# A gated cross-attention and mixture-of-experts block on one core: head pairs scored as two 64-row halves, both norms' rows turned by DMA, and the router in three bf16 parts

## The reference, cut to what matters

```python
x = x + tanh(g_xattn) * xattn(layernorm(x), ctx)        # x: 32 blocks of 128 rows x 512, fp32
x = x + tanh(g_ffn)  * ffn(layernorm(x))
# xattn, 16 heads, per block of 128 rows:
#   q_r = ((xn @ Wq.T) per head @ w_kc_q) @ W_qr        64 numbers a head
#   k_r = rope(ctx) @ W_kr                              64 numbers a head
#   attn = softmax(q_r k_r^T);  ctx_c = attn @ rope(ctx)
#   out  = (ctx_c @ w_kc_kv^T) @ Wo.T
# ffn: logits = xn @ router (512 x 8); the best 2 of 8 experts a row, 1280 slots an expert,
#   silu(gate) * up, down (352 hidden); plus a shared MLP (1408 hidden) for all rows
```

## Time and profile before

| | |
|---|---|
| time, 3 runs | 2081.36 us median (2079.42 to 2082.54) |
| the profiled execution | 2080.16 us, of which its span is 2078.2 us |
| granted TensorE clock, mean over the span | 0.988 of full speed |
| PE, busy share of the span | 96% |
| DVE, ACT, POOL | 49%, 34%, 28% |
| DMA queue of SP, share of the 16 engines | 30.7% |

### The profile page before, as it was taken

The page is one execution under the profiler, slowest core; times in us unless marked ns, Lnnn a source line. Parts: engine busy times, 40 slices in busy tenths (PEclk is TensorE's granted clock), DMA queues, the critical chain, the costliest instruction groups (busy, mean ns, idle before and its releaser), DMA issues.

```text
span 2078.2 us, 32183 instructions
## 1 busy us (share of the span) xinstructions
PE 1998.2 (96%) x11660; PEld 1170.0 (56%) x11844; DVE 1010.4 (49%) x2011; ACT 710.2 (34%) x1969; POOL 576.1 (28%) x653
## 2 busy tenths in 40 slices
PE   7799999999999999989997999999999999999999
PEld 7466666666666666544444555555554444444444
DVE  5766666666666666636532222222223433242343
ACT  4655555555555566522011222222210000000000
POOL 5633333333333354310011433343302210110101
PEclk9999999999999999999998999999999999999999
DMA  8211111111111131141309998989952731221202
GB/s 279 67 43 49 49 49 48 48 48 48 48 48 48 56 104 57 41 123 46 103 22 209 213 223 216 220 216 223 210 123 77 140 93 36 87 81 26 76 16 87
DMA packets 257551, 207.71 MB, mean 100 GB/s; under 512 B 190640, under 2 KB 196528, under 8 KB 257456
## 3 DMA queue, kind: packets, MB, share of 16 engines
q1 hardware_dynamic: 245936, 168.64, 30.7%
q0 software_dynamic: 11520, 37.76, 6.5%
HBM read 113.02 MB, written 48.23 MB: 78 GB/s over the span
## 4 chain that ended last, share of the span: by engine, by line
PE 83%; DVE 7%; issue 4%; ACT 4%; DMA 1%; POOL 1%; SPq 0%; DVEq 0%; ACTq 0%; POOLq 0%
PE o L552 12%; PE score L705 11%; PE o L789 7%; PE score L778 7%; PE p_bank L606 6%; PE p_bank L705 5%; PE o L716 5%; PE m_bank L705 5%; PE p_bank L778 3%; PE m_bank L778 3%; DVE arena L985 3%; PE c_bank L565 3%; PE score L583 3%; PE t_bank L716 3%; PE c_bank L716 3%
## 5 line engine op out<-in xcount | busy, mean ns | idle before, releaser
L552 PE MATMUL o<-arena 128*128 128x512 bf16 x1472 | 339.0, 379 | 14.8 <-DVE arena L985 12.0
L1363 POOL TENSOR_TENSOR arena<-arena 128x512 f32<-128x512 f32 x128 | 133.5, 1043 | 426.4 <-DVE arena L1001 424.6
L552 PEld LDWEIGHTS o<-arena 128*128 128x128 bf16 x1536 | 148.5, 99 | 169.7 <-DVE arena L985 17.3
L705 PE MATMUL score<-arena 128*128 128x512 bf16 x1035 | 235.5, 381 | 2.5 <-issue 0.7
L825 ACT ACTIVATE arena<-score,arena 128x128 f32<-128x128 f32 x512 | 181.3, 366 | 161.4 <-DVE arena L1025 160.2
L985 DVE TENSOR_TENSOR arena<-p_bank,arena 64x512 bf16<-64x512 f32 (+1 forms) x184 | 126.9, 690 | 141.2 <-ACT arena L875 120.0
L606 PE MATMUL p_bank<-arena 128*128 128x256 bf16 x1536 | 178.8, 273 | 1.8 <-DVE arena L985 1.8
L705 PEld LDWEIGHTS score<-arena 128*128 128x128 bf16 x1056 | 103.6, 98 | 128.0 <-issue 4.1
L778 PE MATMUL score<-arena 128*128 128x352 bf16 x960 | 152.4, 316 | 14.5 <-DMA arena<-arena 14.5
L789 PE MATMUL o<-arena 128*128 128x512 bf16 (+1 forms) x680 | 160.9, 381 | 4.2 <-DMA arena<-arena 2.1
L606 PEld LDWEIGHTS p_bank<-arena 128*128 128x128 bf16 x1536 | 150.4, 98 | 21.0 <-issue 1.7
(11 more groups left out here) (166 smaller groups left out, 3164.0 us busy)
## 6 DMA issues: line engine op xcount, KB each, us to landing
xrow_d<-arena SPq DMA_DIRECT2D x80, 256.0 KB, 3.3
arena<-w_expert SPq DMA_DIRECT2D x32, 544.0 KB, 4.9
arena<-w_shared SPq DMA_DIRECT2D x22, 384.0 KB, 3.6
arena<-x SPq DMA_DIRECT2D x16, 512.0 KB, 3.8
arena<-x SPq DMA_DIRECT2D x32, 256.0 KB, 3.8
x_d<-arena SPq DMA_DIRECT2D x32, 256.0 KB, 2.0
xn_d<-arena SPq DMA_DIRECT2D x32, 256.0 KB, 2.1
arena<-x_d SPq DMA_DIRECT2D x8, 1024.0 KB, 5.8
```

What stands on the lines that cost most here:

```text
L552: mm = pe.matmul(o_bank[b % 2][:, :], lhsT=cT[:, a, h, :], rhs=M_w[:, w, 4 * hg + h, :], start=(hg == 0 and n == 0), stop=(hg == 3 and n = ...
L705: mm = pe.matmul(dst[:, :], lhsT=wsh[m][:, a, col:col + P], rhs=xs[g % 2][:, w, t, :], start=(n == 0), stop=(n == 3 * KT - 1))
L1363: pool.tensor_tensor(prob[:, u % 4], prob[:, u % 4], rden[:, u % 4, :].unsqueeze(2).broadcast_to([P, 4, S]), ALU.mult).then_inc(normed, 1)
```

## The change

- The scores of two units are made together in the even steps. `kT` holds K without the zeros; per head one matmul of 64 rows and 128 columns, the even heads from rows 0 to 63 into `score_bank[0]`, the odd ones from rows 64 to 127 into `score_bank[1]`, in turn. Heads are numbered by `head_of` accordingly. The K pieces' high and low parts become one instruction each over 128 rows, and the memsets of `kblk` go.
- PE's fp32 transposes of both norms go. The first norm's rows are split in two bf16 parts (ACT, DVE) at m = 2 and turned by DMA at m = 3. The second's are split in three parts (ACT, POOL, ACT, POOL) at m = 2 to 4, stored, and turned by DMA at m = 5, 6.
- The router is split in three bf16 parts once; a block's logits are 12 bf16 matmuls of 24 columns, whose three groups of 8 columns DVE sums at m = 7 and 0.
- On SP, the experts' first three turns are issued before the stores of `add_shared(1)`; the turned shared tile and the sum come three expert steps later.
- DVE's last two attention steps stand behind its `hidden(0)`.

```diff
 @ SP, step
+                if m == 3:
+                    g = k // 8 + 2
+                    if within(g, NG):
+                        for s in range(2):
+                            wait(sp, xn1_lo, 2 * g + s + 1, 4, it)
...
+                            sp.dma_start_transpose(
+                                xT1[g % 2].rearrange("p l t n -> p (l t) n")[:, :, s * S:(s + 1) * S],
+                                xn1_rows[s].rearrange("p l n -> p (l n)")).then_inc(xT1_in[g % 2], 16)
-                if m in (6, 7):
-                    b = 2 * (k // 8 - 1) + m - 6
+                if m in (5, 6):
+                    b = 2 * (k // 8 - 1) + m - 5
                     if within(b, NB):
-                        wait(sp, ln_lo["l2"], b + 1, 4, it)
+                        wait(sp, xn2_lo, b + 1, 4, it)
...
+                        sp.dma_start_transpose(xT2[b % 2].rearrange("p l t n -> p (l t) n"),
+                                               xn2_rows[b % 2].rearrange("p l n -> p (l n)"))\
+                            .then_inc(xT2_in[b % 2], 16)
 @ SP, before the experts
-            for t in range(4):
-                sp.wait_ge(y_done, 4 + t + 1)
-                sp.dma_start(y_d[4 + t], y_sb[:, t, :]).then_inc(y_out, 16)
-            sp.wait_ge(gu_mm, 22)
+            for k in range(-2, 1):
+                expert_step(k, None)
+            for t in range(4):
+                sp.wait_ge(y_done, 4 + t + 1)
+                sp.dma_start(y_d[4 + t], y_sb[:, t, :]).then_inc(y_out, 16)
+            for k in range(1, 4):
+                expert_step(k, None)
             load_xs(3, None)
 @ PE, step
-                if within(u, NU):
+                if within(u, NU) and u % 2 == 0:
-                    wait(pe, exped, u - 1, 16, it)
+                    wait(pe, exped, u, 16, it)
...
+                    for i in range(4):
+                        mp = 2 * hg + i
                         for n, (a, w) in enumerate(PASSES):
+                            for s in range(2):
+                                rows = slice(s * R, (s + 1) * R)
+                                mm = pe.matmul(score_bank[s][:, i * S:(i + 1) * S], lhsT=qT[g % 2][rows, a, mp, cols],
+                                               rhs=kT[g % 2][rows, w, mp, cols], start=(n == 0), stop=(n == 2))
 @ PE, misc: the transposes at m = 2 to 5 go
-                        wait(pe, ln_up["l2"], b + 1, 4, it)
-                        for t in range(KT):
-                            mm = pe.matmul(m_bank[:, 0:E], lhsT=xT32[:, b % 2, t * P:(t + 1) * P],
-                                           rhs=router_sb[:, t * E:(t + 1) * E], start=(t == 0), stop=(t == KT - 1))
+                        wait(pe, xT2_in[b % 2], 16 * (b // 2 + 1), 32, it)
+                        for n in range(3 * KT):
+                            mm = pe.matmul(m_bank[:, 0:3 * E], lhsT=xT2[b % 2][:, n // KT, n % KT, :],
+                                           rhs=router_w[:, n % KT].rearrange("p w e -> p (w e)"),
+                                           start=(n == 0), stop=(n == 3 * KT - 1))
 @ ACT, end of a step
+                if m == 2 and within(c + 2, NG):
...
+                    for s in range(2):
+                        wait(act, xn1_ready, 2 * g + s + 1, 4, it)
+                        act.copy(xn1_rows[s][:, HI, :], x_ln[:, s, :]).then_inc(xn1_hi, 1)
+                if m in (3, 4):
...
+                        wait(act, xn2_rest, b + 1, 4, it)
+                        act.copy(xn2_rows[b % 2][:, 1, :], xn2[:, b % 2, :]).then_inc(xn2_mid, 1)
 @ DVE, after the piece
+                if m == 2 and within(c + 2, NG):
+                    for s in range(2):
+                        wait(dve, xn1_hi, 2 * (c + 2) + s + 1, 4, it)
+                        lower(xn1_rows[s][:, LO, :], x_ln[:, s, :], xn1_rows[s][:, HI, :]).then_inc(xn1_lo, 1)
 @ POOL
+                if m in (3, 4):
...
+                        wait(pool, xn2_mid, b + 1, 4, it)
+                        pool.tensor_tensor(xn2_rows[b % 2][:, 2, :], xn2[:, b % 2, :], xn2_rows[b % 2][:, 1, :],
+                                           ALU.subtract).then_inc(xn2_lo, 1)
+                if m in (2, 3):
...
+                        wait(pool, xn2_hi, b + 1, 4, it)
+                        pool.tensor_tensor(xn2[:, b % 2, :], xn2[:, b % 2, :], xn2_rows[b % 2][:, HI, :],
+                                           ALU.subtract).then_inc(xn2_rest, 1)
```

More of the change, by code:

```diff
@@ L80, in build @@
         table_sb = words(4 * P)
-        router_sb = words(KT * E)
+        router_sb = words(KT * E).rearrange("p (t e) -> p t e", t=KT)
+        router_w = halves(words(KT * 3 * E // 2)).rearrange("p (t w e) -> p t w e", t=KT, w=3)
         gate_sb = words(2)
@@ L108, in build @@
               for g in range(2)]
-        kblk = [halves(k_region[:, g * 4096:(g + 1) * 4096]).rearrange("p (l m b n) -> p l m b n", l=2, m=NPAIR, b=2)
-                for g in range(2)]
+        kT = [halves(k_region[:, g * 2048:(g + 1) * 2048]).rearrange("p (l m n) -> p l m n", l=2, m=NPAIR)
+              for g in range(2)]
         xT1_region = words(2 * KT * 256)
@@ L135, in build @@
         x_ln = words(2 * D).rearrange("p (b n) -> p b n", b=2)
-        xn1 = words(2 * D).rearrange("p (b n) -> p b n", b=2)
+        xn1_rows = [halves(words(D)).rearrange("p (l n) -> p l n", l=2) for _ in range(2)]
         x1 = words(2 * D).rearrange("p (b n) -> p b n", b=2)
@@ L139, in build @@
         xn2 = words(2 * D).rearrange("p (b n) -> p b n", b=2)
-        xT32 = words(2 * D).rearrange("p (b n) -> p b n", b=2)
-        xn2_rows = [halves(words(D)).rearrange("p (l n) -> p l n", l=2) for _ in range(2)]
+        xn2_rows = [halves(words(3 * D // 2)).rearrange("p (l n) -> p l n", l=3) for _ in range(2)]
+        xT2 = [halves(k_region[:, 4096 + i * 768:4096 + (i + 1) * 768]).rearrange("p (l t n) -> p l t n", l=3, t=KT)
+               for i in range(2)]
         stats = words(4 * 6).rearrange("p (c n) -> p c n", c=4)
@@ L422, in _ @@
             load_a(0)
-            step(-22, None)
+            sp.dma_start(x_ln, x_g[0]).then_inc(xln_in, 16)
             load_a(1)
@@ L616, in step @@
                 misc(k, it)
-            def misc_free(t1, b, bl, it):
-                for s, c, top in ((ln_lo["l1"], t1, NB), (ln_up["l2"], b, NB), (lg_up, bl, NB)):
-                    wait(pe, s, min(c, top) if it is None else c, 4, it)
             def misc(k, it):
@@ L1061, in step @@
                     dve.bn_stats(stats[:, b % 2, :], x1[:, b % 2, :]).then_inc(stat2, 1)
+                if m in (7, 0):
+                    b = 2 * (c - 1) if m == 7 else 2 * c - 3
+                    if within(b, NB):
+                        wait(dve, lg_mm, b + 1, 4, it)
+                        parts = m_bank[:, 0:3 * E].rearrange("p (w e) -> p e w", w=3)
+                        dve.tensor_reduce(logits[:, b, :] if it is None else logits[:, bass.ds(at(b, 4, it), 1), :],
+                                          parts if it is None else parts.unsqueeze(1), AX.X, ALU.add)\
+                            .then_inc(lg_up, 1)
                 if m == 6 and within(c + 3, NG):
@@ L1154, in _ @@
                 lower_b(n)
-            run_steps(dve, step)
+            dve.wait_ge(const_in, 64)
+            for i in range(3):
+                ins = dve.tensor_copy(router_w[:, :, i, :], router_sb)
+                ins.then_inc(router_split, 1)
+                if i < 2:
+                    dve.wait_ge(router_split, 2 * i + 1)
+                    dve.tensor_tensor(router_sb, router_sb, router_w[:, :, i, :], ALU.subtract)\
+                        .then_inc(router_split, 1)
+                    dve.wait_ge(router_split, 2 * i + 2)
+            run_steps(dve, step, LAST_STEP - 2)
             def hidden(v, it):
@@ L1277, in _ @@
             hidden(0, None)
+            for k in range(LAST_STEP - 1, LAST_STEP + 1):
+                step(k, None)
+            dve.wait_ge(lg_mm, NB)
+            dve.tensor_reduce(logits[:, NB - 1, :], m_bank[:, 0:3 * E].rearrange("p (w e) -> p e w", w=3), AX.X,
+                              ALU.add).then_inc(lg_up, 1)
             hidden(1, None)
```

145 lines of the change are left out of this document (47 added, 98 removed).

## The result

| | before | after |
|---|---|---|
| time | 2081.95 us, median of 4 (2079.42 to 2082.55) | 2131.08 us, median of 4 (2125.76 to 2133.06) |
| ratio | | 1.0235 [1.0222, 1.0248] |
| span of the profiled execution | 2078.2 us | 2131.2 us |
| granted clock over the span | 0.988 | 0.970 |

The account below looks back on a forecast made before the run. Attention was taken to go by PE's instruction list, plus a hole before the experts. Attention -13, experts -12, start +3, last steps +1.5, shared-weight splitting +2.5 sum to -18: 2063 us, range 2052 to 2076.

Parts of the forecast that it names:

- At m = 7 the router fills it: Attention, odd step m = 7: the router product covers PE's wait for `cT`, which at m = 5 is 0.45 us.
- The prediction's own sign of being wrong: Router or Q piece waiting over 1.5 us each group, a group below 49.5, or an experts' hole over 6 us.
- D: Rival at the experts' start: another wait stands behind the first, -4 instead of -12 us, 2071 us; chance 0.06.
- The hole before the experts: PE's 14.54 us idle before the experts: earlier turns were to save 12 us (bounds 9 and 14).
- Start: Group 1's first norm goes by casts, subtraction and turn before PE needs it: +3 us (0 to 6).
- C: Rival in the scores: the array's halves don't run together; 2082 us, or 2110 at the far end; chance 0.12.
- B: Rival in attention: turns land late for the router at m = 6 and Q piece at m = 4; 2098 us; chance 0.15.
- Attention's turns: Norm turns by DMA: landing taken as 4.6 us after issue for the first norm, 5.2 for the second.
- The waits for `cT`: PE's `o` after odd steps, with less cover, waits 1.25, 0.7 and 0.45 us at m = 1, 3, 5.
- S: One batch of 24 half-array score matmuls for two units in even steps: 1.0 us, range 0.66 to 1.64.
- R: One block's router product, 12 matmuls of 24 columns in attention: taken as 0.4 us, far end 0.80.
- rival A: Attention's waits stay small: a group of 48.0 us gives 2022 us, half of that gain 2043; chance 0.17.

Follow-up runs that it names:

- e1: The changed kernel with DVE's sum of the first block's logits moved from last to first in its step m = 7; 2074.54 us, ratio 0.9979.
- e9: The changed kernel with PE's attention loop from step 17 to 32 instead of 16 to 31, sum still late; 2089.06 us, ratio 1.0041.
- e5: The early sum's kernel (e1) with 128 increments of an unused semaphore ahead of PE's program; 2055.0 us, ratio 0.9894.
- e10: The changed kernel with the early sum, the shared tile's turn and sum's load behind all experts' steps, and PE's loop at step 17; 2033.85 us, ratio 0.9769.
- e6: The kernel before with only halved scores and full-height K pieces, plus 128 semaphore increments ahead of PE's program; 2084.51 us, ratio 1.0031.
- e7: The changed kernel with the early sum, the late shared turn and load, and 128 increments ahead of PE's program; 2044.59 us, ratio 0.9844.
- e3: The kernel before with one added PE wait at m = 7, ahead of the router, for DVE's low part of the K piece; 2144.48 us, ratio 1.0308.

## Why the prediction was wrong

**The failed step: "At m = 7 the router fills it".** I listed what PE waits for after the cover shrinks: `cT` at m = 1, 3, 5, POOL's division and the turn at m = 6. The second router product was priced as work (0.4) without a look at what frees its bank. Before, too, `m_bank` held one block's logits after the other's, and ACT (857) freed it. What frees it is now DVE's sum at the end of its step, and PE is there 2.9 us earlier. The rows say 42.4 us; mending it alone moved 56.5 us (e1). With the loop mended it is worth 45 to 48: e9 and e5, less e5's 13.7, lie 47.8 apart, and e9 and e10, on one chip, 55.2, of which 10.4 are the late turn. Forecast: 0. The prediction's own sign of being wrong, a router that waits over 1.5 us a group, came true, but for DVE and not for the turn's DMA.

**A cost outside the sum: the loop's reload.** 42 us by e9 in the kernel with the late sum, 33 with the early one (e1 against e5 less 13.7). Of the 42, PE's idle time at the edges is 24.7; the rest goes with half clock, behind the edges and behind the late wait of a group between (5.28 us instead of 2.75 for twelve `o` at 361.16). e5 and e6 show that it hangs on the place of PE's loop in its program. No step of mine spoke of instructions other than by their durations; the change moved the body, and also made it longer (1521 to 1652 instructions, through the halves' 24 matmuls for 12). Turns and router aren't needed for it: e6 has neither. Whether the shorter body has a bad place too wasn't tried; by the estimate above it has none. No row of the kernel before warned of it in attention.

**D was the right sort of rival at the wrong place.** I looked for another wait behind the first at the experts' start. It came 35 us later, with the moved turn and load: 6.53 us and a half clock behind it, 8 in all, 10.4 by e5 against e7.

These three, 42 + 45 + 10.4, are the 97 us between the change and e10. That they close is no check by itself: 42 and 55.2 are steps of one chain from the change by e9 to e10. What held, and what only seemed to:

- The hole before the experts, -11.7 (-12).
- Start +2.7 (+3), by chance: e1 and e10 have the same start on PE and reach unit 0 at 95.0 and 94.9, as before (94.90). In the profiled run of the change a piece at 89.31 ran at half clock (5.00 us instead of 2.79).
- C falls: the halves run together, 24 in 0.77.
- B falls: PE's router waited twice for a turn's DMA, 0.7 us in all. Attention's turns landed 3.3 us (first norm) and 4.3 us (second) after issue in the median, where I took 4.6 and 5.2.
- The waits for `cT` are there, but smaller: at m = 1, 3 and 5 0.46, 0.39 and 0.31 in e10 (at 494.31, 506.38 and 518.37) instead of 1.25, 0.7 and 0.45. With S 0.77 and R 0.31 the work is 46.3 a group instead of 47.4. So the group of e10 is 48.5, not 50.8, and even without the three costs the forecast (2052 to 2076) would have been too slow: e10's 2034 lies on the way to rival A, whose group was 48.0.

**Left open.** Why 2.7 us of waiting in e3 brought PE to half clock each time, and 2.9 in e9 not once in eleven waits up to 707 us, but behind each of the next three, from 762 to 870 us (4.44 us instead of 2.75 for twelve `o` at 762.61). Over 300 to 700 us the granted clock is 0.95 in e3 and 1.00 in e9; nothing was tried on it. Nor was it tried why a back edge idles 5.6 us in e1 and 2.1 in e6 with nearly the same packets.

## What to carry to other kernels

When a product becomes shorter or an engine arrives earlier, list for each of its writes what frees the bank, and where in its engine's step that instruction stands; a reduction of 0.17 us at the end of a step cost 45 to 48 us here. When a wait reads `issue` at intervals of a loop's length, look at the instruction queue's packets: if they recur, move the loop's first step or its length before judging the change itself. Here that alone was 42 us of 2131 in one kernel, 33 and some 14 in two others, so a comparison of two such kernels can be off by up to 2% in either direction.

## What was not expected of the hardware

- 128 more instructions ahead of PE's program turned the reload on in one kernel (1 to 34 packets, +27.5 us with their own 13.7) and off in another (32 to 1, -19.5, again with their own 13.7).
- 128 semaphore increments ahead of PE's program delayed its first matmul by 13.7 us, from 6.7 to 20.4. As PE had waited for a load until 6.7, an increment takes between 0.11 and 0.16 us (an estimate: 13.7 and 20.4 over 128).
- A pair of 64-row matmuls of 128 columns starts every 0.064 us (24 in 0.77), a little above half of a full-height one of 256 columns (0.11).
